# Group loops without jumps, and four moves on VectorE and TensorE, in a two-layer vision transformer with routed experts

## The reference

```python
h = tok(x)                                  # patches @ W.T + b, a class token, + pos_enc
h = h + attn0(layernorm(h))                 # 16 heads of 16, causal, relative bias
h = h + ffn0(layernorm(h))                  # see below
h = h + attn1(layernorm(h))                 # 16 heads of 16, causal
h = h + ffn1(layernorm(h))                  # silu(x @ wg.T) * (x @ wu.T) @ wd.T, int weights / 127

def ffn0(x):                                # width 704, 7 routed experts, the top 2 of them
    probs = softmax(x @ wr.T + rb)
    scores, idx = top_k(probs, 2); scores = scores / scores.sum(-1)
    w = sum(scores * one_hot(idx))
    out = expert(x, sg, su, sd)             # shared expert
    for e in range(7):
        out = out + w[..., e] * expert(x, rg[e], ru[e], rd[e])
    return out
```

## Time and profile before

| what | us |
|---|---|
| median of three runs (1155.06 to 1158.81) | 1158.16 |
| the profiled execution | 1156.55 |
| its span, first to last instruction | 1154.7 |
| TensorE busy (89% of the span) | 1025.2 |
| VectorE busy (54%) | 623.2 |
| ScalarE busy (54%) | 625.2 |
| GpSimd busy (35%) | 403.6 |
| mean granted TensorE clock | 0.95 |

### The profile page before, as it was taken

The page is one execution under the profiler, slowest core; times in us unless marked ns, Lnnn a source line. Parts: engine busy times, 40 slices in busy tenths (PEclk is TensorE's granted clock), DMA queues, the critical chain, the costliest instruction groups (busy, mean ns, idle before and its releaser), DMA issues.

```text
span 1154.7 us, 29051 instructions
## 1 busy us (share of the span) xinstructions
PE 1025.2 (89%) x10676; PEld 922.5 (80%) x10677; DVE 623.2 (54%) x1176; ACT 625.2 (54%) x1087; POOL 403.6 (35%) x298
## 2 busy tenths in 40 slices
PE   6989889979998886999999999994599899799998
PEld 5867768768888886898889889883478677689998
DVE  2436646664444554666666666661267567634343
ACT  3346657754455443655655655562366578646552
POOL 1143434445755551121122122124445354612110
PEclk9999989989999897999999999998789899989999
DMA  6620000017111126011011111103210000000000
GB/s 226 217 79 3 4 3 3 3 47 288 36 26 25 23 45 234 30 36 32 32 36 32 32 36 34 34 33 115 65 44 24 24 3 2 3 1 22 21 12 32
DMA packets 31027, 57.70 MB, mean 50 GB/s; under 512 B 13084, under 2 KB 22506, under 8 KB 29780
## 3 DMA queue, kind: packets, MB, share of 16 engines
q1 hardware_dynamic: 15800, 38.55, 10.4%
q0 software_dynamic: 13328, 10.66, 3.4%
q10 hardware_dynamic: 1804, 7.11, 1.6%
HBM read 41.51 MB, written 14.67 MB: 49 GB/s over the span
## 4 chain that ended last, share of the span: by engine, by line
PE 64%; issue 12%; ACT 9%; DVE 5%; POOL 4%; DMA 3%; ACTq 2%; DVEq 0%; SPq 0%; POOLq 0%
PE ps L1264 23%; PE ps L1269 12%; PE ps L1271 11%; PE ps L1270 11%; PE ps L1417 3%; POOL routed_in L493 2%; ACT shared L823 2%; PE ps L1406 2%; ACTq L253 2%; DMA routed_in<-vts,slot 1%; DVE Hd L1079 1%; DMA routed_in<-prs,slot 1%; ACT shared L825 1%; ACT tile_w L831 1%; ACT Sg L784 1%
## 5 line engine op out<-in xcount | busy, mean ns | idle before, releaser
L517 POOL DMA_INDIRECT routed_out<-yt,tile_to x43 | 65.5, 1523 | 289.9 <-DVE yt L1199 289.9
L1177 DVE TENSOR_TENSOR tile_w<-arena,tile_w 128x1408 fp32r<-128x1408 f32 x86 | 139.3, 1621 | 49.2 <-ACT tile_w L831 49.2
L1264 PE MATMUL ps<-arena,shared 128*128 x516 | 122.6, 387 | 10.2 <-ACT shared L825 10.2
L1269 PE MATMUL ps<-tile_w,xTs 128*128 128x352 f32 x344 | 124.1, 361 | 5.3 <-DVE xTs L1182 5.3
L831 ACT ACTIVATE tile_w<-arena 128x1408 fp32r x86 | 118.4, 1377 | 15.0 <-issue 14.8
L1264 PEld LDWEIGHTS ps<-arena,shared 128*128 128x128 f32 x516 | 94.5, 190 | 31.1 <-issue 20.0
L818 ACT ACTIVATE shared<-ps 128x352 f32<-128x352 f32 x86 | 39.3, 456 | 137.6 <-PE ps L1271 137.6
L1270 PE MATMUL ps<-tile_w,xTs 128*128 128x352 f32 x344 | 112.5, 327 | 0.0
L1271 PE MATMUL ps<-tile_w,xTs 128*128 128x352 f32 x344 | 112.4, 327 | 0.0
L1079 DVE TENSOR_TENSOR Hd<-Sg,ps 128x296 f32<-128x296 f32 x96 | 44.4, 462 | 119.0 <-ACT Sg L784 115.5
L393 POOL TENSOR_TENSOR Km<-KT,cst 128x592 f32<-128x592 f32 x64 | 75.8, 1186 | 86.2 <-PE ps L1264 66.6
(11 more groups left out here) (195 smaller groups left out, 2858.3 us busy)
## 6 DMA issues: line engine op xcount, KB each, us to landing
arena<-in_ew_dram SPq DMA_DIRECT2D x5, 2176.0 KB
x_in<-in_xT_dram SPq DMA_DIRECT2D x7, 888.0 KB, 5.6
xt<-routed_in SPq DMA_DIRECT2D x43, 129.0 KB, 2.1
arena<-in_ew_dram ACTq DMA_DIRECT2D x2, 2176.0 KB, 10.6
yg<-routed_out SPq DMA_DIRECT2D x8, 512.0 KB
out_dram<-h SPq DMA_DIRECT2D x8, 296.0 KB, 2.7
routed_in<-zero_x SPq DMA_DIRECT2D x13, 129.0 KB
qkv_w<-in_qkv_dram ACTq DMA_DIRECT2D x2, 768.0 KB, 9.7
```

What stands on the lines that cost most here:

```text
L517: pool.indirect_dma_start(ys, bass.IndirectOffsetOnAxis(tile_to[b][:, 0:1], 0), yt[b][:], None).then_inc(s_yt, 16)
L1177: dve.tensor_tensor(tile_w[half][1], gate_up_of(w, half), tile_w[half][0].bitcast(F32), ALU.subtract).then_inc(s.wl, 1)
L1264: return pe.matmul(out_, lhsT, rhs, start=start, stop=stop)
L1269: pe.matmul(out_, w[1], x[0], start=start, stop=False)
```

## The change

1. The three group loops become Python loops: groups 1 to 4 are straight code on all engines.
2. On DVE, the second `residual` of a group moves behind `centred(n + 4, 0)`.
3. On DVE, in layer 1, the two `add_routed` move ahead of `values(n, 0)`.
4. At the start of layer 1, only group 0's additions stand ahead of the first mean; group 1's transposes and additions follow it, in banks 2 and 3.
5. In the feed-forward of layer 0, `slots_of(g + 1)` moves from behind gate 5 to behind gate 4, and the last three links of `route` move behind it. `logits` waits for the links up to the slots alone (`ROUTE` is now 13, `SLOTS` 5, and three more). For group 0 the last three links move from the end of attention to behind `slots_of(0, 0)`.

```diff
--- before.py
+++ after.py
@@ -275,9 +275,8 @@
         def over_groups(eng, step):
 
             step(0, 0, True, True, False)
-            with eng.Fori(0, (GROUPS - 4) // 2) as i:
-                for k in (1, 2):
-                    step(2 * i + k, k % 2, False, True, False)
+            for g in range(1, GROUPS - 3):
+                step(g, g % 2, False, True, False)
             step(GROUPS - 3, 1, False, True, False)
             step(GROUPS - 2, 0, False, False, False)
             step(GROUPS - 1, 1, False, False, True)
@@ -287,9 +286,8 @@
 
             first, body, late, near, last = ORDERS[l]
             step(0, 0, first)
-            with eng.Fori(0, (GROUPS - 4) // 2) as i:
-                for k in (1, 2):
-                    step(2 * i + k, k % 2, body)
+            for g in range(1, GROUPS - 3):
+                step(g, g % 2, body)
             step(GROUPS - 3, 1, late)
             step(GROUPS - 2, 0, near)
             step(GROUPS - 1, 1, last)
@@ -468,9 +466,8 @@
 
                 first, body, late, near, last = ORDERS[l]
                 step(0, 0, first, 1 if l == 1 else None)
-                with pool.Fori(0, (GROUPS - 4) // 2) as i:
-                    for k in (1, 2):
-                        step(2 * i + k, k % 2, body, i + 2 if l == 1 else None)
+                for g in range(1, GROUPS - 3):
+                    step(g, g % 2, body, (g + 3) // 2 if l == 1 else None)
                 step(GROUPS - 3, 1, late, None)
                 step(GROUPS - 2, 0, near, None)
                 step(GROUPS - 1, 1, last, None)
@@ -880,6 +877,7 @@
                                   ALU.subtract).then_inc(s.cen, 1)
 
             routing = F[0]
+            first_routes = []
             R = slice(0, W2)
             done = [0]
 
@@ -926,13 +924,15 @@
                 yield
                 link(dve.tensor_tensor(t(5), t(7), wide(3), ALU.is_equal))
                 link(dve.tensor_tensor(t(10), t(4), t(5), ALU.add))
+                assert done[0] == ROUTE
                 yield
+                link = linker(RCHAIN * g + ROUTE + SLOTS)
                 dve.wait_ge(routing.r_ex, g + 1)
                 link(dve.tensor_scalar(c(1), c(9), 1.0, None, ALU.add))
                 dve.wait_ge(routing.sent, g + 1)
                 link(dve.reciprocal(rows_x[b][:, :, 0, D], c(1)))
                 link(dve.tensor_tensor(rows_x[b][:, :, 1, D], rows_x[b][:, :, 0, D], c(9), ALU.mult))
-                assert done[0] == ROUTE
+                assert done[0] == RCHAIN - ROUTE - SLOTS
                 yield
 
             def slots_of(g, b):
@@ -947,7 +947,7 @@
                 link(dve.tensor_reduce(slot_f[:], at, AX_X, ALU.add))
                 link(dve.tensor_copy(slot[b][:], slot_f[:]))
                 link(dve.tensor_tensor(place[:], place[:], ps[:, 6, 32:32 + EXPERTS], ALU.add))
-                assert done[0] == RCHAIN - ROUTE
+                assert done[0] == SLOTS
 
             def attention(l):
                 a = A[l]
@@ -1008,10 +1008,12 @@
 
                 first, body, late, near, last = ORDERS[l]
                 if l == 1:
-                    for g in range(2):
-                        for c in range(DK):
-                            add_routed(g, c, 6 + c)
+                    add_routed(0, 0, 6)
+                    add_routed(0, 1, 7)
                 centre(a, 0, 6)
+                if l == 1:
+                    add_routed(1, 0, 2)
+                    add_routed(1, 1, 3)
                 dve.wait_ge(a.xn, FREE + 1)
                 centre(a, 1, 6)
                 scaled(0, 0)
@@ -1024,10 +1026,10 @@
                     if not X.first:
                         normalise(g - 1, n - 1, 3, 1 - b, X.bank("O3"))
                     greatest(n + 1, 1)
-                    values(n, 0, X.bank("V0"))
                     if X.comb:
                         add_routed(g + 2, 0, X.bank("comb0"))
                         add_routed(g + 2, 1, X.bank("comb1"))
+                    values(n, 0, X.bank("V0"))
                     centred(n + 1, 1)
                     values(n + 1, 1, X.bank("V1"))
 
@@ -1053,10 +1055,10 @@
                     normalise(g, n + 2, 2, b, X.bank("O2"))
                     if not X.last:
                         greatest(n + 4, 0)
+                    if not X.last:
+                        centred(n + 4, 0)
                     if not X.first:
                         residual(g - 1, 1, X.bank("out1p"))
-                    if not X.last:
-                        centred(n + 4, 0)
                 over_body(dve, l, step)
                 normalise(GROUPS - 1, 4 * GROUPS - 1, 3, 1, last.bank("O3"))
                 if l == 0:
@@ -1066,7 +1068,7 @@
                 residual(GROUPS - 1, 0, last.bank("out0"))
                 residual(GROUPS - 1, 1, last.bank("out1"))
                 if l == 0:
-                    next(routes)
+                    first_routes.append(routes)
 
             def gates(l, s, g, rows):
 
@@ -1152,11 +1154,12 @@
                     for j in gates(l, s, g, hidden_chunks((I0, I1)[l])):
                         if l == 0 and first and j == 0:
                             slots_of(0, 0)
+                            next(first_routes[0])
                         if l == 0 and not last:
-                            for _ in range(((0, 1, 2, 1) if first else (1, 1, 1, 1))[j] if j < 4 else j - 4):
+                            if j == 4:
+                                slots_of(g + 1, 1 - b)
+                            for _ in range((0, 1, 2, 1, 1, 0)[j] if first else (1, 1, 1, 1, 1, 0)[j]):
                                 next(routes)
-                            if j == 5:
-                                slots_of(g + 1, 1 - b)
                         if l == 0 and last and j < TABLE_PIECES:
                             next(pieces)
                         if j == 1 and not first:
@@ -1453,13 +1456,13 @@
                 if l == 1:
                     pe.sem_inc(C.mm0, FREE)
                     pe.sem_inc(C.mm1, FREE)
-                    for g in range(2):
-                        for c in range(DK):
-                            if g == 1:
-                                pe.wait_ge(C.h, c + 1)
-                            routed_out(g, g, c, 6 + c)
-                    pe.wait_ge(C.h, 4)
+                    routed_out(0, 0, 0, 6)
+                    routed_out(0, 0, 1, 7)
+                    pe.wait_ge(C.h, 2)
                 mean(a, 0, 6)
+                if l == 1:
+                    routed_out(1, 1, 0, 2)
+                    routed_out(1, 1, 1, 3)
                 if l == 0:
                     embed(GROUPS - 2, 0)
                 variance(a, 0, 7)
@@ -1468,6 +1471,8 @@
                 pe.wait_ge(a.cen, FREE + 1)
                 if l == 0:
                     pe.wait_ge(emb_cp, FREE + GROUPS)
+                else:
+                    pe.wait_ge(C.h, 4)
                 mean(a, 1, 6)
                 pe.wait_ge(s_lower, 2 * l + 1)
                 project(0, 0, 0, 2)
@@ -1591,7 +1596,7 @@
                             if l == 0:
                                 counts(0)
                         if routing and j == (1 if first else 0):
-                            pe.wait_ge(s.r, RCHAIN * (g + 1))
+                            pe.wait_ge(s.r, RCHAIN * g + ROUTE + SLOTS)
                             logits(g + 1, 1 - b, 6)
                         if routing and j == 0:
                             pe.wait_ge(s.rowB, FREE + g + 1)
@@ -1694,8 +1699,9 @@
             ffn(1)
 
 
-ROUTE = 16
-RCHAIN = ROUTE + 5
+ROUTE = 13
+SLOTS = 5
+RCHAIN = ROUTE + SLOTS + 3
 TABLE_PIECES = 4
```

## The result

The changed kernel takes **1111.45 us** (median of 4 runs, 1109.31 to 1115.27) beside 1157.25 us for the kernel before on the same chip (4 runs, 1155.06 to 1158.81): a ratio of 0.9607, 95% interval 0.9586 to 0.9628, which is 45.5 us less by that ratio. The prediction said 1116 us, 1108 to 1132. The profiled execution of after is its slowest, 1115.27 us with a span of 1113.4.

What follows compares the result with a forecast made beforehand. TensorE was taken as the pace-maker, with time to win only in its pauses and clock falls. Terms of 17.1 + 4.2 + 2.6 + 3.3 + 14.0 = 41.2 us gave 1116 us, range 1108 to 1132.

Steps and rivals of the forecast that it cites:

- The loops: Attention of both layers: writing loops out removes TensorE's taken jump and what follows it; 17.1 us, 11.2 to 17.5.
- Residual: Attention scores: DVE's subtraction starts about 0.35 us sooner in twelve places; 4.2 us, 0 to 6.2.
- Added choices: Layer 1, ahead of the projections: TensorE's pauses for `add_routed` nearly vanish; 2.6 us, 0 to 3.2.
- start of layer 1: Start of layer 1: TensorE's first mean waits only for group 0's additions; 3.3 us, 1 to 3.4.
- Slots: First feed-forward stage: `logits` no longer waits for the slots, GpSimd's scatters limit the gain; 14 us, 10 to 15.9.
- rival A: Feed-forward stage gives 10 us or less, TensorE and GpSimd pushing each other, smaller parts half; 1125 us, chance 0.20.
- Rival B: Feed-forward stage: `logits` waits for the normalised group instead; 0 to 6 us from this part, near 1127 us, chance 0.09.
- Rivals C and D: Attention. C: straight code stalls on TensorE, 1170 us, chance 0.03. D: jump not the cause, 1132.5 us, chance 0.03.

Runs made afterwards that it cites:

- lower_early: The changed kernel with GpSimd's `xf_lo` of the next group put between the sixth and seventh scatter transfers, in layer 0's feed-forward; 1119.76 us, ratio 0.9660.
- both_late_early: The changed kernel with GpSimd's landing wait behind the next group's first two transfers, and `xf_lo` between the sixth and seventh; 1103.86 us, ratio 0.9543, fastest found.
- landing_late: The changed kernel with GpSimd's wait for a group's scattered rows moved behind the first two transfers of the next group; 1106.57 us, ratio 0.9554.
- ffn_loops_back: The changed kernel with only the feed-forward loop put back on every engine, attention loops still written out; 1111.41 us, ratio 0.9594.

## Why the prediction was right

**The loops** (17.1 us, 11.2 to 17.5). 18.8 by the ratio of the kernel with them alone, in its trace 7.7 in layer 0 and 7.9 in layer 1 (9.8 and 7.8 with TensorE's loop alone). The mechanism stood as told: TensorE's branch, the pause behind it and the clock after them. What TensorE does in the 2.23 us behind the branch is not shown. The layers were sized unevenly: layer 1's group of 22.48 us, which I left out, fell to 21.11 as well, and in layer 0 the first group came out 1.3 us longer.

**Residual** (4.2 us). The pause shrank by 0.30 us, not 0.35, in all twelve places: 3.6 us. The kernel with it alone gained 6.9 (interval 4.4 to 9.6), so the term was too small; 1.3 us of the rest stands in the groups around the jump of layer 0.

**Added choices** (2.6 us, 0 to 3.2) gave 3.2 in the traces, all of the wait of the earlier trace rows, and the **start of layer 1** (3.3 us) 4.1 in the kernel with the orders, 2.7 in after against the profile of before. That profile had 27.8 us for this stretch, the four others with the old order 29.1 to 29.2.

**Slots** (14 us, 10 to 15.9). 14.4 by the kernel with them alone; 17.0 in its trace and 12.1 in that of after. The sizing rested on GpSimd's chain of 19.39 us a group with two pauses of 4.1. The trace shows 18.72 and 19.27 us for undisturbed groups, and both pauses. Two groups without a pause came out at 22.34 and 21.66 us for a reason the sum lacked: GpSimd's `xn` waited 4.92 and 4.10 us for ScalarE's `rsd`, which comes behind TensorE's variance.

```profile
307.67 1.47 POOL L407 TENSOR_TENSOR xf_lo<-xn,xf_hi 128x592 fp32r<-128x592 f32 x1
314.07 1.48 POOL L401 TENSOR_TENSOR xn<-cen,rsd 128x592 f32<-128x592 f32 x1 [4.92 <-ACT rsd L601]
...
324.47 1.35 POOL L490 DMA_INDIRECT routed_in<-vts,slot  x1 [4.41 <-issue]
```

That is rival A's mechanism, the two chains pushing each other, at a smaller price: the last scatter came 12.1 us earlier against the start of the stage where I had 15.3, and the clock still fell to 0.81 in one step (0.93 in the step of the earlier trace rows). Rival A left 10 us or less of this part; 14.4 were measured. That GpSimd's chain is the longer one was right: `lower_early` lengthened it, and the kernel got slower. Rival B (another wait in the slots' place) came true only in part: the new wait is for `xf_lo`, 6.4 us, not for the norm, and removing it at GpSimd's cost made the kernel 8 us slower. Rivals C and D did not happen.

The sum of 41.2 us fits the two traces (41.3) better than the result (45.5). The profiled execution of after is 3.8 us above its median, that of before 0.7 us below the 1157.25 of the comparison. That the two sums meet within 0.1 us is luck: in the table the routing stage gave 1.9 us less than forecast, layer 1's attention 2.0 more, and the stretches taken at 0 gave 1.4 and 1.3 and took 1.6. By the kernels with one part each, the forecast was low by 1.7 us for the loops, 0.4 for the slots and 4.0 for the three orders together (14.1 measured, 10.1 forecast); the intervals of these ratios are 5 to 8 us wide.

## What to carry to other kernels

Price a taken jump by the group around it, not by the branch: the branches and the pause behind one of them were 11 us here, and the slower groups around them cost about half as much again. Here it was TensorE's jump that counted; its queue written out gave all that four queues did. Where two engines are both nearly full, find the longer chain by lengthening it on purpose: the edit that looked like a gain for TensorE cost 8 us, and pointed at GpSimd's chain, where a later wait for the rows then paid.

## What the runs showed of the hardware

**A VectorE instruction can be held until two of GpSimd's have ended.** Moved one gate ahead, slots and weights now run when GpSimd issues the last transfer of a group and then does `xf_lo` and `xn` back to back. The second line of the slots, of after: eight executions, least, median and most in ns; then one of them in the timeline of VectorE, and GpSimd's beside it.

```profile
L946 DVE TENSOR_TENSOR rt<-rt x8: 211/214/3507, 249.2 to 395.9; 74x56 f32<-74x56 f32 x8
```

```profile
333.71 3.51 DVE L946 TENSOR_TENSOR rt<-rt 74x56 f32<-74x56 f32 x1
337.26 0.21 DVE L947 TENSOR_REDUCE slot_f<-rt 74x8 f32<-74x56 f32 x1
```

```profile
332.90 1.35 POOL L490 DMA_INDIRECT routed_in<-vts,slot  x1 [0.30 <-issue]
334.28 1.46 POOL L407 TENSOR_TENSOR xf_lo<-xn,xf_hi 128x592 fp32r<-128x592 f32 x1
335.70 1.45 POOL L401 TENSOR_TENSOR xn<-cen,rsd 128x592 f32<-128x592 f32 x1
```

It takes 3.51 us where it otherwise takes 0.21, and ends with GpSimd's second instruction (335.70 + 1.45 = 337.15). In before the same line took 211 to 214 ns in all eight executions. VectorE's busy time in the stage rose from 90.81 to 106.57 us with the same 299 instructions, the two windows above show it. Six instructions of slots and weights in it, of 1.36 to 3.75 us where others of their lines take 0.16 to 0.21, make up some 13 us of that.

The Trainium skill, "SBUF — State Buffer", section SBUF: two separate sides, describes such a collision: the two engines share one pair of ports, and whichever starts first has it for its whole instruction; this concerns a VectorE instruction in a mode with two ports, or one with two inputs in SBUF against a GpSimd one that reads SBUF. The trace agrees in that the instruction, which has two inputs in SBUF, is held. It does not bear out who goes first: VectorE's instruction starts 0.57 us ahead of `xf_lo` in the record, while the last transfer is being issued, and is held to the end of `xn`. Whether that transfer plays a part is not shown. The hold is not confined to two inputs: L931 has one, and lasts 1.38 us where it otherwise takes 0.17, to the end of the `xn` of 314.07 us.

```profile
314.19 1.38 DVE L931 TENSOR_SCALAR rt<-rt 74x4 f32<-74x4 f32 x1
```

I had counted slots at gate 4 as eight short links. What the collision costs the kernel is not shown: in the fastest kernel VectorE is at 99.21 us, but that kernel differs in other ways.

**GpSimd's pause of 4.1 us is not a matter of the count of transfers alone.** Before and after have it once every 26 transfers (4.40 in the earlier trace rows; 4.41 and 4.13 in after). In the two kernels that wait for the landing behind the second transfer it does not occur in the stage at all, though they issue as many. In `both_late_early` the only idle time over 1 us ahead of a transfer from the second group on is this wait, once, and one for the weights:

```profile
273.17 1.34 POOL L491 DMA_INDIRECT routed_in<-vts,slot  x1 [2.31 <-DMA routed_in<-prs,slot]
387.00 1.43 POOL L491 DMA_INDIRECT routed_in<-vts,slot  x1 [2.60 <-DVE vts L940]
```

So part of what the late wait gave may be these two pauses, and not only the landing off the chain. From the first to the last group's first transfer GpSimd takes 151.95 us in after and 140.51 in `landing_late`, 11.4 less, and the two pauses are some 8 us of that; `ffn_loops_back`, which has both pauses, takes 145.81. Its waits for the landing are mostly gone too, but in their place come waits for `rsd`, 12.3 us in four places against 9.0 in two. No run tells the two gains apart.
